# A two-layer block with routed experts on one core: one copy of the experts' sums, with shared rows added into the next pair

## The reference, cut to what matters

```python
x = x + _layernorm(attention(_layernorm(x)))          # x: 8 x 512 x 256, 16 query heads on 4 key heads
x = x + _layernorm(ffn(_layernorm(x)))

def ffn(hidden):                                      # T = 4096 tokens, H = 256, F = 176
    scores = softmax(x @ gate_w.T)                    # 64 experts
    topk_w, topk_idx = top_k(scores, 6)
    # each expert takes its first CAP = 64 tokens, in the order of the tokens
    g = silu(einsum('ech,ehf->ecf', buf, w_gate))
    u = einsum('ech,ehf->ecf', buf, w_up)
    d = einsum('ecf,efh->ech', g * u, w_down)         # 64 rows of 256 for each expert
    y = sum over a token's experts of d * topk_w      # a token beyond CAP adds nothing
    return y + (silu(x @ sh_gate.T) * (x @ sh_up.T)) @ sh_down.T
```

## Time and profile before

| | us |
|---|---|
| median of 3 runs | 1392.39 |
| the profiled execution, its own time | 1392.17 |
| its span in the profile | 1390.1 |
| PE (TensorE) busy in the span | 1304.2 |
| DVE (VectorE) busy | 1109.6 |
| ACT (ScalarE) busy | 855.3 |
| POOL (GpSimd) busy | 793.7 |

### The profile page before, as it was taken

The page is one execution under the profiler, slowest core; times in us unless marked ns, Lnnn a source line. Parts: engine busy times, 40 slices in busy tenths (PEclk is TensorE's granted clock), DMA queues, the critical chain, the costliest instruction groups (busy, mean ns, idle before and its releaser), DMA issues.

```text
span 1390.1 us, 26790 instructions
## 1 busy us (share of the span) xinstructions
PE 1304.2 (94%) x8603; PEld 1142.8 (82%) x8603; DVE 1109.6 (80%) x3652; ACT 855.3 (62%) x2322; POOL 793.7 (57%) x1054
## 2 busy tenths in 40 slices
PE   6999999999999999999999999999999998798850
PEld 5898999999999999999999999999998988654420
DVE  7778787889788987998788978897889897744438
ACT  6677666666666666666566666666666664544324
POOL 5666565556565655556555646565556553746644
PEclk9999999999999999999999999999999999999985
DMA  9100000100010001000100000000100017989986
GB/s 296 64 1 16 1 17 9 43 16 17 5 39 24 17 1 43 24 1 16 43 24 1 16 28 26 15 16 9 36 23 16 1 38 208 273 254 289 293 256 260
DMA packets 50506, 96.48 MB, mean 69 GB/s; under 512 B 4705, under 2 KB 36930, under 8 KB 50370
## 3 DMA queue, kind: packets, MB, share of 16 engines
q1 hardware_dynamic: 44226, 85.33, 19.1%
q0 software_dynamic: 6144, 9.44, 3.3%
HBM read 68.27 MB, written 26.49 MB: 68 GB/s over the span
## 4 chain that ended last, share of the span: by engine, by line
PE 84%; DVE 5%; POOL 4%; DMA 3%; issue 3%; ACT 1%; POOLq 0%; DVEq 0%
PE bank_t L708 18%; PE bank_s L708 17%; PE bank_o L708 16%; PE bank_y L708 13%; PE bank_f L708 8%; PE bank_t L794 4%; PE bank_s L794 4%; POOL ffn_sums L2144 2%; PE bank_f L794 2%; DMA ffn_sums<-dsum,idx_s 2%; POOL xg L2131 1%; DVE fstat L1905 1%; DVE fa L1900 1%; DVE fa L1925 1%; DMA xg<-token_table,idx_g 0%
## 5 line engine op out<-in xcount | busy, mean ns | idle before, releaser
L1973 POOL TENSOR_TENSOR prob<-prob,rinv 128x512 f32<-128x512 f32 (+3 forms) x512 | 362.0, 725 | 250.9 <-DVE rinv L1514 250.5
L1114 ACT ACTIVATE prob<-prob,negmax 128x512 f32<-128x512 f32 (+3 forms) x512 | 283.2, 555 | 19.9 <-DVE negmax L1501 13.7
L1960 POOL TENSOR_TENSOR q_l<-q_sum,q_h 128x128 fp32r<-128x128 f32 x254 | 182.8, 741 | 107.9 <-ACT q_h L1094 105.0
L708 PE MATMUL bank_y<-wo_h,o_h 128*128 128x256 f32 x512 | 146.8, 287 | 1.9 <-DVE o_l L1526 1.9
L708 PE MATMUL bank_y<-wo_l,o_h 128*128 128x256 f32 x512 | 142.9, 279 | 0.0
L708 PE MATMUL bank_y<-wo_h,o_l 128*128 128x256 f32 x512 | 142.8, 279 | 0.0
L1127 ACT ACTIVATE pt_h<-bank_t 128x256 fp32r<-128x256 f32 (+3 forms) x208 | 89.8, 432 | 80.5 <-PE bank_t L794 73.1
L708 PE MATMUL bank_o<-pt_h,v_h 128*128 128x512 f32 (+1 forms) x384 | 136.6, 356 | 2.4 <-DVE o_l L1526 2.4
L1127 ACT ACTIVATE pt_h<-bank_s 128x512 fp32r<-128x512 f32 (+3 forms) x203 | 88.2, 434 | 79.4 <-PE bank_s L794 74.2
L708 PE MATMUL bank_o<-pt_l,v_h 128*128 128x512 f32 (+1 forms) x384 | 136.7, 356 | 0.0
L708 PE MATMUL bank_o<-pt_h,v_l 128*128 128x512 f32 (+1 forms) x384 | 136.0, 354 | 0.0
(11 more groups left out here) (461 smaller groups left out, 4047.0 us busy)
## 6 DMA issues: line engine op xcount, KB each, us to landing
w_gu<-in_w_in SPq DMA_DIRECT2D x32, 704.0 KB
w_dn<-in_w_out SPq DMA_DIRECT2D x32, 320.0 KB
xio<-in_x SPq DMA_DIRECT2D x16, 512.0 KB, 4.6
token_table<-rows SPq DMA_DIRECT2D x8, 640.0 KB, 3.7
ffn_sums<-keys SPq DMA_DIRECT2D x4, 1024.0 KB
x_rows<-xio SPq DMA_DIRECT2D x8, 512.0 KB, 2.9
ffn_sums<-ytr SPq DMA_DIRECT2D x16, 256.0 KB, 2.2
fx<-x_rows SPq DMA_DIRECT2D x8, 512.0 KB, 6.9
```

The lines of the kernel that those rows point to most:

```text
L708: return pe.matmul(o, l, r, start=start, stop=stop, skip_group_check=True)
L1114: act.activation(p_, p_, ACT.Exp, bias=negmax[:, r, i:i + 1], scale=-1.0, accum_out=rsum[:, r, i:i + 1]).then_inc(exp_made, 1)
L1960: pool.tensor_tensor(l_[:, cols], sum_of(step)[:, cols], plain(h_)[:, cols], ALU.subtract).then_inc(pos_low, 1)
L1973: pool.tensor_tensor(p_, p_, rinv[:, r, i:i + 1].to_broadcast([P, (i + 1) * P]), ALU.mult).then_inc(prob_made, 1)
```

## The change: what it does

There is one copy of the sums. A token that pair j and pair j+1 both have is left out of the scatter of pair j (its row goes to a spare row), and its finished row is added, by a product on TensorE, to its row in pair j+1. So two scatters that follow one another never hold the same token row, and both may be under way. Spare rows differ for even and odd pairs. For that each pair needs its own targets one step earlier (`own_same`, `own_targets`), a product that lays the next pair's targets along a row (`own_row`), a 128 x 128 comparison (`again`), its maximum by row (`moved`), and the product `add_again`. ScalarE's `expert_out(j)` waits for `add_again(j-1)` in place of the down product itself. `same` has three buffers in place of two.

```diff
-    sums = nc.dram_tensor("ffn_sums", [2 * SUMROWS, E], F32, kind="Internal").ap()
+    sums = nc.dram_tensor("ffn_sums", [SUMROWS, E], F32, kind="Internal").ap()
...
-            zero_left, per, n0 = 2 * SUMROWS - NT, ZERO_PER, NT
+            zero_left, per, n0 = SUMROWS - NT, ZERO_PER, NT
...
-            AHEAD_SUMS = 2
-            for copy in range(2):
-                sp.wait_ge(dma_s[copy], 16 * (NP // 2))
-                for b in range(AHEAD_SUMS):
-                    load_sums(b, copy)
-            for b in range(AHEAD_SUMS, NB):
-                for copy in range(2):
-                    load_sums(b, copy)
+            for parity in range(2):
+                sp.wait_ge(dma_s[parity], 16 * (NP // 2))
+            for b in range(NB):
+                load_sums(b)
...
+            def own_row(j):
+
+                if j > 2:
+                    pe.wait_ge(again_made, j - 2)
+                pe.wait_ge(own_made, j + 1)
+                pe.matmul(bank[f"y{j % 2}"][:, EC * P:(EC + 1) * P], slots[:, 1, j:j + 1].to_broadcast([P, P]), ident[:],
+                          start=True, stop=True, skip_group_check=True).then_inc(row_in, 1)
+
+            def add_again(j):
+
+                pe.wait_ge(again_made, j + 1)
+                pe.wait_ge(d_made, j + 1)
+                mm(bank[f"t{(j + 1) % 2}"][:, 0:E], again[j % 2][:], dsum[j % ND][:], stop=True).then_inc(again_in, 1)
...
                 if j + 2 < NP:
                     expert_turn(j + 2)
+                if j + 1 < NP:
+                    own_row(j + 1)
                 if j:
                     add_second(j - 1)
                 expert_out(j)
+                if j:
+                    add_again(j - 1)
...
-                act.wait_ge(down_in, j + 1)
+                if j:
+                    act.wait_ge(again_in, j)
+                else:
+                    act.wait_ge(down_in, 1)
...
+            def own_targets(j):
+
+                at_ = slice(CAP, 2 * CAP)
+                done(dve.tensor_reduce(twice[j % 2][at_, :], same[j % 3][at_, :], AX, ALU.max))
+                dve.scalar_tensor_tensor(out=slots[at_, 1, j:j + 1], in0=twice[j % 2][at_, :],
+                                         scalar=slots[at_, 2, j:j + 1], in1=slots[at_, 1, j:j + 1],
+                                         op0=ALU.mult, op1=ALU.add).then_inc(own_made, 1)
+
             def targets(j):
...
+                dve.wait_ge(row_in, j + 1)
+                if j > 1:
+                    dve.wait_ge(again_in, j - 1)
+                dve.tensor_scalar(again[r][:], bank[f"y{(j + 1) % 2}"][:, EC * P:(EC + 1) * P], slots[:, 1, j:j + 1],
+                                  None, ALU.is_equal).then_inc(again_made, 1)
+                dve.wait_ge(again_made, j + 1)
+                done(dve.tensor_reduce(moved[r][:], again[r][:], AX, ALU.max))
+                dve.scalar_tensor_tensor(out=idx_s[:, j:j + 1], in0=moved[r][:], scalar=slots[:, 2, j:j + 1],
+                                         in1=slots[:, 1, j:j + 1], op0=ALU.mult, op1=ALU.add
                                          ).then_inc(target_made, 1)
...
             for j in range(NP):
+                if not j:
+                    own_same(0)
+                    own_targets(0)
                 expert_act(j)
+                if j < LAST_PAIR:
+                    own_targets(j + 1)
                 targets(j)
 
-            def add_sums(b):
-                dve.wait_ge(dma_f[b], 32)
-                dve.tensor_tensor(fa[b][:], fa[b][:], fb[b][:], ALU.add).then_inc(sum_dve, 1)
-
             def statistics(b):
-                dve.wait_ge(sum_dve, b + 1)
+                dve.wait_ge(dma_f[b], 16)
```

More of the change, by code:

```diff
@@ L64, in build @@
     x2_runs = x2_dram.rearrange("(b p i) e -> b p i e", p=P, i=TT)
-    sum_runs = [sums[a * SUMROWS:a * SUMROWS + NT, :].rearrange("(b p i) e -> b p i e", p=P, i=TT)
-                for a in range(2)]
+    sum_runs = sums[0:NT, :].rearrange("(b p i) e -> b p i e", p=P, i=TT)
     out_runs = out.rearrange("b (p i) e -> b p i e", p=P)
@@ L99, in build @@
         key_row = place("key_row", [P, HT], F32)
-        copy_at = place("copy_at", [P, 2], F32)
+        slot_row = place("slot_row", [P, 2 * CAP], F32)
         causal = place("causal", [P, T], F32)
@@ L209, in build @@
         aside2 = place("aside2", [P, 2 * CAP], F32)
-        second = place("second", [P, 3, NP], F32)
-        same = [place(f"same{i}", [P, CAP], F32) for i in range(2)]
+        slots = place("slots", [P, 3, NP], F32)
+        same = [place(f"same{i}", [P, CAP], F32) for i in range(3)]
         twice = [place(f"twice{i}", [P, 1], F32) for i in range(2)]
+        again = [place(f"again{i}", [P, P], F32) for i in range(2)]
+        moved = [place(f"moved{i}", [P, 1], F32) for i in range(2)]
         idx_g = place("idx_g", [P, NP], I32)
@@ L231, in build @@
         assert at[0] <= end_at, (at[0], end_at)
-        at[0] = weights_at
-        fb = [place(f"fb{b}", [P, TT, E], F32) for b in range(NB)]
-        assert at[0] <= weights_end
         at[0] = work_at
@@ L680, in sync_program, with load_sums @@
                 sp.dma_start(fx[b][:], x2_runs[b]).then_inc(dma_x2in, 16)
-            def load_sums(b, copy):
-                sp.dma_start((fa, fb)[copy][b][:], sum_runs[copy][b]).then_inc(dma_f[b], 16)
+            def load_sums(b):
+                sp.dma_start(fa[b][:], sum_runs[b]).then_inc(dma_f[b], 16)
             def store_out(b, parts=1):
@@ L1846, in vector_program @@
             last.then_inc(gather_made, 1)
-            dve.tensor_copy(idx_s[0:CAP, :], turned[0:CAP, 1, :, 0])
-            at_ = slice(CAP, 2 * CAP)
-            dve.tensor_copy(second[at_, 0:2, :], turned[at_, 0:2, :, 1])
-            dve.tensor_scalar(second[at_, 2, :], turned[at_, 2, :, 1], -1.0, None, ALU.mult).then_inc(index_made, 1)
+            for u in range(2):
+                at_ = slice(u * CAP, (u + 1) * CAP)
+                dve.tensor_copy(slots[at_, 0:2, :], turned[at_, 0:2, :, u])
+                last = dve.tensor_scalar(slots[at_, 2, :], turned[at_, 2, :, u], -1.0, None, ALU.mult)
+            last.then_inc(index_made, 1)
             dve.wait_ge(index_made, 1)
@@ L1855, in vector_program, with own_same @@
             dve.tensor_tensor(low[:, n, :], made, plain(high[:, n, :]), ALU.subtract).then_inc(a_low[lane_], 1)
-            def targets(j):
-                r, at_ = j % 2, slice(CAP, 2 * CAP)
-                done(dve.tensor_reduce(twice[r][at_, :], same[r][at_, :], AX, ALU.max))
-                dve.scalar_tensor_tensor(out=idx_s[at_, j:j + 1], in0=twice[r][at_, :], scalar=second[at_, 2, j:j + 1],
-                                         in1=second[at_, 1, j:j + 1], op0=ALU.mult, op1=ALU.add
+            def own_same(j):
+                at_ = slice(CAP, 2 * CAP)
+                if not j:
+                    dve.wait_ge(dma_firsts_in, 32)
+                if j > 2:
+                    dve.wait_ge(same_in, j - 2)
+                k, m = divmod(j, NP // 2)
+                dve.tensor_scalar(same[j % 3][at_, :], firsts[k][at_, m, :], slots[at_, 0, j:j + 1], None,
+                                  ALU.is_equal).then_inc(same_made, 1)
+                dve.wait_ge(same_made, j + 1)
@@ L1877, in expert_act @@
                 dve.wait_ge(gate_tanh, j + 1)
-                dve.scalar_tensor_tensor(out=x_, in0=x_, scalar=1.0, in1=gate, op0=ALU.add, op1=ALU.mult)
-                if j > 1:
-                    dve.wait_ge(same_in, j - 1)
-                at_ = slice(CAP, 2 * CAP)
-                if not j:
-                    dve.wait_ge(dma_firsts_in, 32)
-                k, m = divmod(j, NP // 2)
-                dve.tensor_scalar(same[r][at_, :], firsts[k][at_, m, :], second[at_, 0, j:j + 1], None,
-                                  ALU.is_equal).then_inc(same_made, 1)
-                dve.wait_ge(same_made, j + 1)
+                dve.scalar_tensor_tensor(out=x_, in0=x_, scalar=1.0, in1=gate, op0=ALU.add, op1=ALU.mult).then_inc(gated_made, 1)
+                if j < LAST_PAIR:
+                    own_same(j + 1)
                 if j > 1:
                     dve.wait_ge(act_turned, j - 1)
+                dve.wait_ge(gated_made, j + 1)
                 dve.scalar_tensor_tensor(out=ag[r][:], in0=x_, scalar=half_w[r][:], in1=up, op0=ALU.mult,
```

41 lines of the change are left out of this document (24 added, 17 removed).

## The result

The changed kernel takes 1401.72 us (median of 5, 1401.14 to 1401.79), the kernel before beside it 1392.39 (5 executions, 1388.14 to 1395.69). The ratio is 1.0073, with an interval of 1.0058 to 1.0088: slower, by 0.6 to 0.9%. The forecast was 1400.4.

The account below looks back on a forecast made before the run. TensorE was taken to bound the loop, partly with scatter waits, and VectorE the last stage. 15.2 - 0.5 - 1.2 - 5.0 - 0.5 = +8.0 on 1392.17 gave 1400.2, or 1400.4 for the median; range 1390 to 1409.

Parts of the forecast that it names:

- The mechanism: Loop: work added to TensorE first fills the difference between 4.05 and 3.45 us; what is beyond is paid in full.
- The rival in which the scatters' time covers the products: Loop: products fall in TensorE's idle time, the step stays 3.8 us, the kernel takes 1385.4; chance 0.12.
- break-even of 4.08: Loop step in us at which the whole change, 29T - 118.4, neither gains nor loses.
- The lean rival: Loop: both products at their lower bounds, 0.69 us together, step 4.14, kernel 1394.1; chance 0.18.
- The rule of the Trainium skill: Loop: FP32 products make four passes, so both take 0.64 us, step 4.09, about 8 us faster than the forecast.
- TensorE, +17.1 against +15.2: Loop: `add_again` 0.58 and `own_row` 0.33 us make the step 4.36, the 31 steps 132.3 against 117.15: +15.2.
- VectorE and ScalarE, nothing: Loop: VectorE's added operations are covered by TensorE's longer step and `expert_out`'s 0.58 us later release is not paid: nothing.
- The end of the loop: Last `activations_turn` to the last scatter's issue: a chain of 4.5 us in place of 5.05, -0.5.
- Loading the sums: Behind the last scatter: eight loads in place of sixteen, the first taken as 5.0 us against 6.2, -1.2.
- The last stage: Normalisation behind the loop: without VectorE's sum, 24.8 us to the seventh bias in place of 29.8, -5.0.
- The ring through ScalarE: Last stage: the loop of bias, scaling, residual and next bias sets blocks of 3.4 us.
- The start: Kernel start: zero stores shrink from 4.3 MB to 0.3, freeing a load ScalarE waits for, -0.5 us.

Follow-up runs that it names:

- e1: The kernel before with the two products added to each pair, on constants, into unused columns, nothing waiting for them: 1404.8 us, ratio 1.0107.
- e2: The changed kernel without `add_again` and the waits for it, so shared rows are left out of the second pair's sum: 1388.25 us, ratio 0.9977.
- e4: The changed kernel with the maximum of the shared tokens taken four times, 0.96 us more for VectorE per pair: 1406.28 us, ratio 1.0107.
- e7: The kernel before with the two products on constants added, and `expert_out` waiting for the last product of the step: 1408.27 us, ratio 1.0134.
- e5: The kernel before with the changed kernel's tail: only the first copy of the sums loaded, nothing added to it: 1384.43 us, ratio 0.9945.
- e12: The changed kernel with the row as a transpose, tiles at old addresses, and the last stage's residual behind bias and aggregates: 1392.65 us, ratio 1.0012.
- e6: The changed kernel with the old amount of zero stores, 4.3 MB in place of 0.3: 1402.57 us, ratio 1.0079.
- e11: The changed kernel with `slot_row` behind all other tiles and 32 bytes left in its place, so tiles lie as before: 1399.1 us, ratio 1.0063.
- e10: The kernel before with the second copy added by accumulating DMAs from GpSimd's queue, not VectorE, and the last stage reordered: 1397.67 us, ratio 1.0057.
- e13: The kernel before, VectorE adding the copies of the first four batches and accumulating DMAs those of the last four: 1390.18 us, ratio 0.9984.
- e8: The kernel before with one constant tile made larger, so later tiles lie 480 bytes further on, no instruction different: 1396.17 us, ratio 1.0034.
- e3: The changed kernel with `own_row` as a transpose of the same column, not a product with the identity: 1398.67 us, ratio 1.0067.

## Why the prediction was right

**The mechanism.** It held: what is added to TensorE first fills the difference between 3.45 us and what the scatters allow, and the rest is paid. The changed loop has no free time on TensorE; e1 makes it (133.90 of 134.26 us) with the two products and nothing else; e2 shows the scatters come back as bound when one of them goes. The rival in which the scatters' time covers the products is out: the step is 4.42, beyond the break-even of 4.08. The lean rival is out: the pair of records beside the down product costs 0.64, not 0.46. The rule of the Trainium skill that was weighed, FP8 and Floating Point Precision, section TensorE Precision Notes, would by the prediction's estimate have made the two products 0.64 together; they measured 0.95, and the row's surroundings were the better guide.

**TensorE, +17.1 against +15.2.** `own_row` was forecast 0.33 and is 0.31. `add_again` was forecast 0.58 and is 0.64, plus the 0.11 by which the down product ahead of it is longer (0.92 in e2, 1.02 to 1.03 with either product behind it, in e1 with no semaphore waited for). `expert_turn` gives 0.09 back. The step is 4.42, not 4.36: 29 times that difference is 1.7 us of the 1.9.

**VectorE and ScalarE, nothing.** Right both. VectorE was given 0.8 us to spare ahead of `ag` and 0.9 ahead of `own_row`; in e4 about 0.9 could be used up before the steady step grew. The later release of `expert_out` cost nothing in the loop of e7.

**The end of the loop, +0.5 against -0.5.** This step failed. I worked out TensorE's and ScalarE's chain, and it came as forecast: the last row is ready at 1358.60. But GpSimd begins the scatter at 1359.60, 1.00 later. This time from ScalarE's end to GpSimd's start is missing in the chain, where it stood at nothing. It is no wait for an older scatter, though the code has one for the last scatter of the same parity: the last scatter begins 1.00 or 1.01 us behind ScalarE's end in e1, e2, e4 and the changed kernel, where the scatter of its parity had begun 4.99, 4.85, 6.80 and 6.01 us before. The pair ahead of it in the changed kernel needs 0.76 (1356.48 against 1355.34 + 0.38). Why the last takes 0.24 more stays open.

**Loading the sums, -2.8 against -1.2.** The size was off. I took a landing of 4.6 from loads at the start and rounded up; eight loads behind an idle queue gave 3.36, and 3.22 in e5.

**The last stage, -5.8 against -5.0.** The ring through ScalarE was right: blocks of 3.44, found again in e5 on the old loop. The way to the first bias was shorter than taken, 3.31 us (1370.20 - 1366.89) in place of 4.3, and that is the difference: the 4.3 were read where a GpSimd operation on this way takes 1.11 us beside VectorE's sum, and without the sum it takes 0.23 (shown at the end). In the block where the ring broke (e12) it is 2.84, the 2.9 of VectorE's own sum.

**The start, -0.2 against -0.5.** Near in size by luck. Two effects were in it, one of which I had not thought of: fewer zero stores give about 1 us (e6), and the tiles' new places cost 2.5 (e11). So the gathers' indices are made 1.55 us later than before (1207.57 against 1206.02). The rest hides this: from there to the first turn it is 12.22 us in place of 13.97. In the other kernels this stretch takes 10.6 us (e7) to 14.4 (e6), and kernels with the same instructions in it differ by 2, so that what it gave here is chance as far as the runs show.

**The sum.** +9.2 in the profiled executions, +9.3 in the medians, +8.0 forecast: errors of +1.9, +1.0, +0.3 and +0.5 against -1.6 and -0.8. What stays open is the spread of kernels whose loop waits for scatters: with the same instructions it took 117.15 us in the profile of before, 119.24 in e5, 117.40 in e10, 118.63 in e13 and 121.64 in e8, and the medians of the kernel before over its groups of runs were 1390.99 to 1392.88 with single times from 1385.54 to 1395.69. The loop from which all was reckoned is the shortest of the five, so part of the +17.1 can be chance. The changed kernel, bound by TensorE, spans 0.65 us.

## What to carry to other kernels

Where an engine has waits in only part of its steps, work added to it is free only up to the mean of those waits (here 0.38 us a step: 117.15 us against 3.18 + 29 x 3.45 + 2.04 = 105.27 without waits; the prediction's 0.33 left out that the first and the last step are shorter), and the rest is paid once per step; take its price from a row in the same place and add what it does to the row ahead of it. A second copy that lets transfers overlap can be cheaper than the products which make it needless: here 0.76 + 0.31 us on the bound engine, some thirty times and about two fifths of it covered, stood against 8.6 us once at the end. Compare a kernel whose tiles moved with one whose tiles lie as before, or a fifth of a per cent can be put down to the wrong edit.

## What the hardware showed that was not expected

- **Where tiles lie in the on-chip memory changes the speed.** 480 bytes more ahead of them, no instruction changed: four batches of attention take 588.54 us in place of 587.28 (e8), and the changed kernel goes from 588.43 to 587.34 when they are taken back (e11).
- **A 256-column float32 product with 128 by 128 weights lengthens the product ahead of it** by 0.11 us, whether it waits for a semaphore (the changed kernel) or not (e1). The product ahead has 64-column weights in all of these runs; other neighbours were not tried.
- **A float32 row laid out by a transpose** is one record of 0.27 us in place of two that take 0.39, and a step gains 0.12 (3.6 us in 31 steps, e3).
- **A small GpSimd operation takes 0.23 or 1.11 us by what VectorE does beside it.** On GpSimd, the changed kernel (statistics on VectorE):

```profile
1384.50 0.23 POOL L2019 TENSOR_SCALAR fnw<-fmv 128x4 f32<-128x4 f32 x1 [2.09 <-DVE fmv L1950]
```

and the kernel before (a sum of two 128x1024 tiles on VectorE):

```profile
1370.55 1.11 POOL L1980 TENSOR_SCALAR fnw<-fmv 128x4 f32<-128x4 f32 x1 [1.81 <-DVE fmv L1910]
```

The Trainium skill, GPSIMD Engine Reference, section Specifications, says that GpSimd shares its access to the on-chip memory with VectorE and contends with VectorE's instructions that have two inputs there. The trace agrees and gives the price, here 0.88 us: VectorE's sum runs from 1370.37 to 1371.56, and the operation that began within it ends at 1371.66. In e12, where the residual stands beside it, it takes 1.11 again.
- **An accumulating DMA of 512 KB lands late**: 9.6 us in the median of e10, where the plain loads of the same size beside it take 7.4.
- **Where a loop waits for scatters, its time spreads**: 117.15 to 121.64 us for the same instructions, against 134.20 to 134.26 in three kernels bound by TensorE (the changed kernel, e6, e11).
